# Local attention in a four-layer transformer kernel: the order of two pairs of steps on ScalarE and TensorE

## The reference, cut to what matters

```
def _layer(x, wqkv, qs, ksc, wo, ...):
    h = shift_token(x)
    q, k, v = split(h @ wqkv)                  # 8 heads of 64
    q = l2norm(q) * qs ; k = l2norm(k) * ksc   # norm of each head's 64 values
    q, k = rotary_xpos(q, k)
    o = local_attention(q, k, v)               # window 64, own window and the one before
    x = x + o @ wo
    ...                                        # layer norm and a gated FFN behind it
```

## Time and profile before

| | us |
|---|---|
| median of 3 runs | 2303.07 |
| the runs | 2303.02, 2303.07, 2311.46 |
| the profiled execution | 2294.92 |
| its span (first to last instruction) | 2293.1 |
| TensorE busy | 2136.7 |
| ScalarE busy | 1801.0 |
| VectorE busy | 1706.8 |
| GpSimd busy | 1431.8 |

### The profile page before, as it was taken

One profiled execution on the slowest core, in us unless ns is written; L12 is line 12 of the kernel. 1 busy time (PEld: TensorE's weight loads), 2 busy tenths in 40 slices (PEclk: granted clock), 3 DMA queues, 4 the chain that ended last, 5 costly groups with the idle time before them and its releaser, 6 DMA issues. The chain is left out here.

```text
span 2293.1 us, 67424 instructions
## 1 busy us (share of the span) xinstructions
PE 2136.7 (93%) x22342; PEld 1585.6 (69%) x22342; DVE 1706.8 (74%) x4362; ACT 1801.0 (79%) x6112; POOL 1431.8 (62%) x1432
## 2 busy tenths in 40 slices
PE   6997999998797999999999999898999999999999
PEld 4994666665795888854888854674788864788863
DVE  5565999996555899964899964675899963899964
ACT  4775999995676999973999973556999982999982
POOL 3663777774662888840888850671788850788850
PEclk8997999999899999999999999999999999999999
DMA  6111000000113000000000000000000000000000
GB/s 249 44 42 42 2 0 0 0 1 38 35 44 111 12 7 9 7 3 3 11 7 9 7 0 0 2 0 6 9 9 8 8 1 5 9 9 7 9 1 37
DMA packets 22568, 46.02 MB, mean 20 GB/s; under 512 B 5344, under 2 KB 13664, under 8 KB 22048
## 3 DMA queue, kind: packets, MB, share of 16 engines
q1 hardware_dynamic: 17440, 34.07, 4.4%
q0 software_dynamic: 4992, 10.23, 1.6%
HBM read 24.51 MB, written 11.40 MB: 16 GB/s over the span
## 5 line engine op out<-in xcount | busy, mean ns | idle before, releaser
L280 POOL TENSOR_TENSOR space<-space 128x512 f32<-128x512 f32 x256 | 325.8, 1273 | 270.4 <-DVE space L383 270.1
L275 POOL TENSOR_TENSOR space<-space 128x512 f32<-128x512 f32 x256 | 267.6, 1045 | 128.1 <-ACT space L316 127.6
L330 ACT ACTIVATE space<-psum,space 128x128 f32<-128x128 f32 x1024 | 337.0, 385 | 2.7 <-DVE space L374 2.7
L177 PE MATMUL psum<-big,space 128*128 128x256 f32 x1024 | 267.9, 384 | 7.3 <-issue 3.5
L269 POOL TENSOR_TENSOR space<-space 128x512 f32<-128x512 f32 x256 | 267.0, 1043 | 7.9 <-DVE space L354 7.3
L1008 POOL TENSOR_TENSOR space<-space 128x256 f32<-128x256 f32 (+1 forms) x256 | 221.9, 888 | 75.2 <-DVE space L1117 70.9
L374 DVE TENSOR_REDUCE space<-psum 128x4 f32<-128x512 f32 x256 | 177.1, 692 | 100.8 <-PE psum L192 96.5
L1053 ACT ACTIVATE space<-space 128x128 f32<-128x128 f32 (+1 forms) x512 | 226.1, 446 | 7.3 <-DVE space L1108 6.5
L330 ACT ACTIVATION_READ_ACCUMULATOR space<-psum,space 128x1 f32 x1024 | 201.8, 197 | 0.0
L177 PEld LDWEIGHTS psum<-big,space 128*128 128x128 f32 x1024 | 175.6, 191 | 29.6 <-issue 16.2
L677 ACT ACTIVATE big<-psum,wt 128x512 f32<-128x512 f32 (+1 forms) x96 | 65.4, 686 | 151.9 <-PE psum L654 151.9
(11 more groups left out here) (194 smaller groups left out, 5425.8 us busy)
## 6 DMA issues: line engine op xcount, KB each, us to landing
big<-early SPq DMA_DIRECT2D x1, 6944.0 KB, 27.9
rows<-space SPq DMA_DIRECT2D x16, 256.0 KB, 2.7
z<-token_y SPq DMA_DIRECT2D x16, 256.0 KB, 4.7
space<-z SPq DMA_DIRECT2D x64, 64.0 KB, 1.9
space<-z SPq DMA_DIRECT2D x64, 63.8 KB, 2.1
big<-late SPq DMA_DIRECT2D x1, 3114.0 KB, 13.7
x<-x_t SPq DMA_DIRECT2D x4, 512.0 KB, 6.0
x_final<-x SPq DMA_DIRECT2D x8, 256.0 KB, 2.0
```

The lines of the kernel that those rows point to most:

```text
L177: ins = mm(qk_ps[:, t * T:(t + 1) * T].rearrange("p (n c) -> p n c", n=2), hT[:, k, t * P:(t + 1) * P], wq[:, 0:2, j, :], start=(t == 0), ...
L275: pool.tensor_tensor(x, x, rn[:, (j - 1) % 2, :].unsqueeze(2).to_broadcast([P, 8, LD]), ALU.mult).then_inc(scaled, 1)
L280: pool.tensor_tensor(t3[:, j % 2, :], t1[:, j % 2, :], t2[:, j % 2, :], ALU.add).then_inc(summed, 1)
L330: ins = act.activation(pr[:, j % 2, h, t * P:(t + 1) * P], s_ps[h][:, t * P:(t + 1) * P], ACT.Exp, bias=nm[:, j % 2, h, t:t + 1], accum_ou ...
```

## The change

On ScalarE the norms of unit s-1 (L312, L316) go ahead of the square of unit s (L306); before they stood right behind it. On TensorE the transpositions of unit s-3's weights (L232) go ahead of the output projection of unit s-5 (L221). Waits, signals, operands and buffers of every instruction stay the same.

```diff
@@ tensor_body
-            u = s - 5
-            if runs(u, U):
-                c = (j - 5) % CH
-                pe.wait_ge(o_ready, S0 + u + 1)
-                ...
-                mm(z_ps, wo[:, c, :], oT[:, (j - 5) % 2, :], ...).then_inc(wo_ready, 1)
-
             u = s - 3
             if runs(u, U):
                 pe.wait_ge(normed, S0 + u + 1)
                 ...
                 ins.then_inc(ptp_ready, 1)
+
+            u = s - 5
+            if runs(u, U):
+                c = (j - 5) % CH
+                pe.wait_ge(o_ready, S0 + u + 1)
+                ...
+                mm(z_ps, wo[:, c, :], oT[:, (j - 5) % 2, :], ...).then_inc(wo_ready, 1)
@@ scalar_body
+            u = s - 1
+            if only is None and runs(u, U):
+                act.wait_ge(ss_ready, S0 + u + 1)
+                act.activation(lnn[...], ss[...], ACT.Ln, ...).then_inc(ln_ready, 1)
+                act.wait_ge(ln_ready, S0 + u + 1)
+                if at_least(u, 2):
+                    act.wait_ge(scaled, S0 + u - 1)
+                act.activation(rn[...], lnn[...], ACT.Exp, ...).then_inc(rn_ready, 1)
             if begins(s, only):
                 act.wait_ge(proj_ready, S0 + s + 1)
                 if at_least(s, 2):
                     act.wait_ge(ss_ready, S0 + s - 1)
                 act.activation(sq[:, j % 2, :], qk_ps, ACT.Square).then_inc(sq_ready, 1)
             if only is not None:
                 continue
-            u = s - 1
-            if runs(u, U):
-                ... (the same Ln and Exp)
```

More of the change, by code:

```diff
@@ L233, in tensor_body @@
                 ins.then_inc(ptp_ready, 1)
+            u = s - 5
+            if runs(u, U):
+                c = (j - 5) % CH
+                pe.wait_ge(o_ready, S0 + u + 1)
+                if is_first(u):
+                    prev.free(pe, 7)
+                if c == 0 and at_least(u, CH):
+                    pe.wait_ge(z_ready, B0 + b - 1)
+                mm(z_ps, wo[:, c, :], oT[:, (j - 5) % 2, :], start=(c == 0), stop=(c == CH - 1), skip_group_check=True).then_inc(wo_ready, 1)
             if runs(s, U):
@@ L301, in scalar_body @@
                 act.activation(pt[:, j % 2, :, :].rearrange("p h n -> p (h n)"), pt_ps, ACT.Copy).then_inc(pt_ready, 1)
+            u = s - 1
+            if only is None and runs(u, U):
+                act.wait_ge(ss_ready, S0 + u + 1)
+                act.activation(lnn[:, (j - 1) % 2, :], ss[:, (j - 1) % 2, :], ACT.Ln, scale=float(2 ** 20), bias=g.tiny[:, 0:1]).then_inc(ln_ready, 1)
+                act.wait_ge(ln_ready, S0 + u + 1)
+                if at_least(u, 2):
+                    act.wait_ge(scaled, S0 + u - 1)
+                act.activation(rn[:, (j - 1) % 2, :], lnn[:, (j - 1) % 2, :], ACT.Exp, scale=-0.5, bias=g.tiny[:, 1:2]).then_inc(rn_ready, 1)
             if begins(s, only):
```

## The result

The changed kernel takes 2333.61 us (median of 4 runs, 2333.42 to 2340.54), the kernel before 2304.39 (the three runs above and one more). The ratio is 1.0128 with a 95% interval of 1.010 to 1.0156: 29.2 us slower. The forecast was 2337.3, a loss of 34.2; its range for 8 in 10, 2318 to 2362, holds the result. Lines of the moved instructions in the changed kernel: Ln L305, Exp L309, square L314, the weights' transpositions L222, the output projection L233; the others keep theirs.

A forecast was written before the change was run, and what follows sets the result against it. The prediction took a 3.97 us loop over GpSimd, TensorE and ScalarE as the bound. 244 x (4.11 - 3.97) = +34.2 us on the 2303.07 median gave 2337.3 us; 8-in-10 range 2318 to 2362.

The forecast's parts named there:

- The loop of 3.97 over GpSimd, TensorE and ScalarE: Local attention: scale, transpose, two copies, square, Ln, Exp, back to scale; said to set the old step of 3.97 us.
- Part 1, the new loop: ScalarE's reorder closes a loop L366, L312, L316, L306, L381, L383, L391, L354, L360, L366: 4.11 us a step.
- The other, which I put at 4.08: Second new loop, leaving the first at L306 over ScalarE's L322 and L330 to L354: 4.08 us a step.
- The sum: Total added time: 244 steps x (4.11 - 3.97) = +34.2 us.
- The register work and the turns: Mean local-attention step above the steady one, by register work and hardware-loop turns: 0.03 us, assumed unchanged.
- Part 2, at zero: TensorE's reorder, transpositions ahead of the output projection: price zero, any added wait hidden.
- The wait I bounded at 0.13: TensorE's wait at L232 for GpSimd's L269, after L209's weight loads: 0 to 0.13 us, hidden.
- The faster side: Rival: new loop shorter than thought, ScalarE's own work sets 3.88 a step; -22 us, 2281; 6%.
- "TensorE is the bound": Rival: TensorE, 99.77 busy, holds the step at 3.97 whatever ScalarE does; 2303 us, no change; 6%.
- The third, the transpositions' wait: Rival: L232's 0.13 wait delays v's projection and ScalarE's next step; step 4.24, +66 us, 2369; 6%.
- The sign that I gave for being wrong: VectorE's queue: the distance from L391 to L354 staying 0.40 while the step is longer.
- The rule of the Trainium skill: Improve the fullest engine, ScalarE at 97.70: a reorder could give at most its 2.3% idle time and could cost nothing.

The follow-up runs named there:

- e7: Kernel before, with VectorE's mask copy cut from 256 to 16 columns a bank (rest left out): 2304.57 us, ratio 1.0001.
- e12: Kernel before with only ScalarE's reorder, and the mask copy cut from 256 to 16 columns a bank: 2267.01 us, ratio 0.986.
- e10: Changed kernel with ScalarE's copy L322 on 128 of its 256 columns (other half left out): 2318.67 us, one run.
- e9: Changed kernel with VectorE's multiplication by sine L383 on 256 of its 512 columns (other half left out): 2329.72 us, one run.
- e2: Kernel before with only TensorE's part of the change, ScalarE's order as before: 2304.86 us, ratio 0.9995.
- e1: Kernel before with only ScalarE's part of the change, TensorE's order as before: 2332.80 us, ratio 1.012.
- e8: Changed kernel, with the mask copy cut from 256 to 16 columns a bank (rest left out): 2290.78 us, ratio 0.9953.

## Why the prediction was right, and where its sizes were off

- **What bounds the kernel.** The loop of 3.97 over GpSimd, TensorE and ScalarE was the right reading. e7 (VectorE 0.5 lighter, ratio 1.0001) shows that it is not VectorE, and e12 that cutting the loop frees 1.4% once the mask is out of the way, with TensorE's work as before.
- **Part 1, the new loop.** Right in mechanism and in its chain: the steady step is 4.09, VectorE waits 0.21 for the square (0.2 was forecast), Ln starts 0.04 behind L366. Off in size, by two terms of the loop that I chose. For L391 to L354 I took 0.36, the shortest distance in a row; it was still a wait for L330, and alone it is 0.33 (e10). For L306 I took 0.60; behind Exp it takes 0.58. With those two it is 4.06, and 4.07 as measured in e10, not 4.11. The other, which I put at 4.08 and left aside as the shorter, is the one that sets the pace, at 4.09 (e9). The sum took 0.14 a step; the mean step grew by 0.12, which gives 29 us instead of 34.2. That the time comes out near all the same owes something to the two loops being so close: the one that I took for the longer is not the one that binds.
- **The register work and the turns**, 0.03 a step, I left as it was, and that held: the mean lay 0.03 above the steady step before and lies 0.03 above it after (4.12 against 4.09). No run shows that it is register work; the rows show only that two steps in four are longer.
- **Part 2, at zero.** Right: e2 at 0.9995 and e1 at the full loss. The wait I bounded at 0.13 is larger, 0.25 in the step shown and 63.8 us over 245 places, yet hidden: L222 starts 1.46 behind L366 as I had it, but L209's loads end 1.21 behind it (904.15) and not 1.33. Its cover was the longer step, and e8 against e12 shows the price of TensorE's order without it: some 20 us.
- **The rivals.** The faster side named the right point, whether VectorE idles ahead of L381 for the square: it does. "TensorE is the bound" (no change) falls by the time itself, and by e12, where TensorE does its work in 3.89 a step. TensorE's share is no witness: with the same loss it is 97.09 in the changed kernel and 99.91 in e1. The third, the transpositions' wait, is real but not on the path: e1 is as slow without it. The sign that I gave for being wrong, 0.40 from L391 to L354 in a longer step, did not come: it is 0.35.
- **The rule of the Trainium skill** on occupancy ("Perfetto Trace Analysis", section "Identifying the Most-Contended Engine"), as the prediction reads it, would have had nothing lost. The measurement decides: ScalarE, the fullest of the three, went from 97.70 to 94.41 busy while the kernel got slower.

What stays open: whether a complete kernel can use the order with the norms ahead. e12 shows that it is worth 1.4% if the mask is off VectorE's path, but it leaves most of the mask out, and no place for the mask off that path was tried. To let L381 wait for the projection instead of the square, which would open only the first loop, was not tried; L381 and the square read the same PSUM bank, and no run here shows what happens when nothing orders the two.

## What to carry to other kernels

When every engine is 80 to 100% busy in a software pipeline, write down the loops of one step (from an instruction over waits and queue order back to itself) and compare their lengths; the longest is the pace, and to move an instruction is to take its term out of one loop and put it into others. Check all loops that the moved instruction and its new neighbours lie on, not the one you want to open: moving the norms cut 3.97 and made 4.09, and moving the sum of squares cut 4.09 and made 4.35. A distance between two starts in a full queue may itself be a wait for another engine, so a loop built from such distances is an upper bound until an experiment removes the other wait.

## What the runs showed that was not expected

- Two loops 0.02 apart (4.07 and 4.09) look the same in one timeline. Halving one instruction of each told them apart in two runs.
- With the change the copy L295 is often listed at 0.67 us (median 664 ns) where it took 0.60 (598 ns). It then starts earlier within the copy ahead of it; in e9 L337 runs from 881.98 to 882.47 and L295 starts at 882.28, 0.19 ahead of that end; in the step of the earlier trace rows it starts behind the end of L337 (905.59 + 0.48, against 906.09). The instruction is the same, so a longer listed duration in a full queue need not be more work.
